# Window attention on one core: key differences with features on partitions, and value products summed by TensorE's turns

## The reference

```python
xw  = x.reshape(B, hg, ws, wg, ws, C).transpose(0, 1, 3, 2, 4, 5)     # windows of 2 x 2 positions
qkv = (xw @ Wqkv + bqkv).reshape(B, hg * wg, ws * ws, 3, nh, hd)      # 8 heads of 16 features
attn = softmax(einsum('bgnqd,bgnkd->bgnqk', q, k) * scale, axis=-1)   # 4 queries x 4 keys per window and head
o    = einsum('bgnqk,bgnkd->bgnqd', attn, v)
g = window_attn(xr) @ Wproj + bproj                                   # the full branch
l = resize(blur(window_attn(mean of 2x2 pixels)))                     # the pooled branch, bilinear, back to 32 x 32
out = x + (g + l).transpose(0, 3, 1, 2)
```

## Time and profile before

| | us |
|---|---|
| median of 3 runs | 103.97 |
| span of the profiled execution, first to last instruction | 101.1 |
| TensorE (PE) busy | 87.2 |
| VectorE (DVE) busy | 82.4 |
| GpSimd (POOL) busy | 51.4 |
| ScalarE (ACT) busy | 45.6 |

### The profile page before, as it was taken

How to read it: one execution, slowest core, us unless ns; L and a number is a source line. 1 busy time by engine, 2 the same in 40 slices (tenths; PEclk the granted TensorE clock), 3 DMA queues, 4 the chain that set the end, 5 groups by cost and what they waited for, 6 DMA issues and landing times.

```text
span 101.1 us, 1874 instructions
## 1 busy us (share of the span) xinstructions
PE 87.2 (86%) x647; PEld 79.8 (79%) x647; DVE 82.4 (81%) x137; ACT 45.6 (45%) x99; POOL 51.4 (51%) x43
## 2 busy tenths in 40 slices
PE   4949899989947998799999998589999994999960
PEld 1927589979947996799999996479999983999920
DVE  0062906999989999997979999999999999989770
ACT  3160247935862744864578505851613451222110
POOL 6201004499696930099999369729189549000000
PEclk9999999999998599999999999999999999999998
DMA  1699500000000000000000000005000004000072
GB/s 54 181 406 394 209 0 0 0 6 0 0 0 3 0 3 0 6 0 0 0 0 6 0 0 0 0 0 207 6 0 0 0 0 172 36 6 3 0 306 109
DMA packets 2313, 5.35 MB, mean 53 GB/s; under 512 B 513, under 2 KB 897, under 8 KB 2305
## 3 DMA queue, kind: packets, MB, share of 16 engines
q1 hardware_dynamic: 2016, 4.92, 12.7%
q10 hardware_dynamic: 288, 0.33, 1.1%
HBM read 3.15 MB, written 2.10 MB: 52 GB/s over the span
## 4 chain that ended last, share of the span: by engine, by line
PE 45%; DVE 21%; issue 13%; POOL 9%; DMA 5%; ACT 3%; SPq 0%; DVEq 0%; ACTq 0%; POOLq 0%
PE sm_ps L858 7%; PE ot_ps L882 6%; DVE sm_ps L674 6%; PE k_ps L823 6%; DMA x_sb<-in_x 5%; DVE qk L640 5%; POOL pv L387 5%; PE v_ps L847 5%; PE q_ps L823 3%; PE job_ps L802 2%; POOL qk L387 2%; PE ot_ps L776 2%; DVE out_sb L705 2%; PE v_ps L788 2%; PE ot_ps L788 2%
## 5 line engine op out<-in xcount | busy, mean ns | idle before, releaser
L387 POOL TENSOR_TENSOR pv<-pv 128x1024 f32<-128x1024 f32 (+1 forms) x11 | 21.6, 1964 | 8.3 <-DVE pv L691 7.9
L691 DVE TENSOR_TENSOR pv<-sm_ps,v_sb 128x2048 f32<-128x2048 f32 x9 | 20.6, 2290 | 0.3
L640 DVE TENSOR_TENSOR qk<-q_ps,k_sb 128x512 f32<-128x512 f32 x32 | 20.8, 679 | 0.0
L462 POOL TENSOR_TENSOR qk<-q_sb,k_sb 128x512 f32<-128x512 f32 x8 | 10.3, 1289 | 11.3 <-ACT q_sb L551 8.0
L387 POOL TENSOR_TENSOR qk<-qk 128x1024 f32<-128x1024 f32 (+1 forms) x7 | 15.5, 2217 | 0.2
L858 PE MATMUL sm_ps<-ident,qk 128*128 128x128 f32 x108 | 13.6, 274 | 1.3 <-POOL qk L387 1.2
L858 PEld LDWEIGHTS sm_ps<-ident,qk 128*128 128x128 f32 x108 | 11.9, 141 | 1.8 <-issue 1.7
L882 PE MATMUL ot_ps<-ident,pv 128*128 128x128 f32 x80 | 10.5, 274 | 2.5 <-POOL pv L387 1.9
L882 PEld LDWEIGHTS ot_ps<-ident,pv 128*128 128x128 f32 x80 | 9.0, 141 | 3.7 <-issue 3.3
L674 DVE TENSOR_TENSOR sm_ps<-expd,inv 128x128 f32<-128x128 f32 x10 | 10.1, 1011 | 0.3
L580 ACT ACTIVATE ot<-ot_ps,bias_v 128x512 f32<-128x512 f32 x10 | 6.9, 687 | 7.6 <-PE ot_ps L882 7.6
(11 more groups left out here) (88 smaller groups left out, 146.5 us busy)
## 6 DMA issues: line engine op xcount, KB each, us to landing
x_sb<-in_x SPq DMA_DIRECT2D x3, 512.0 KB, 7.1
out<-out_sb SPq DMA_DIRECT2D x3, 512.0 KB, 2.6
resize_sb<-in_resize SPq DMA_DIRECT2D x1, 640.0 KB, 7.3
x_sb<-in_x SPq DMA_DIRECT2D x2, 256.0 KB, 4.9
out<-out_sb SPq DMA_DIRECT2D x2, 256.0 KB, 2.0
w_sb<-in_L_conv_Wqkv ACTq DMA_DIRECT2D x1, 192.0 KB, 5.6
bias_rows<-in_L_conv_bqkv ACTq DMA_DIRECT2D x1, 128.0 KB, 4.6
wp_sb<-in_L_conv_Wproj SPq DMA_DIRECT2D x1, 64.0 KB, 6.6
```

What stands on the lines that cost most here:

```text
L387: return engine.tensor_tensor(low, low, high, ALU.add)
L462: nc.gpsimd.tensor_tensor(*query_key_operands(n, i, q_sb[:, n % 2, :], i - WIN + POOL_QUERIES), ALU.mult).then_inc(qk_pool, 1)
L640: ins = nc.vector.tensor_tensor(*query_key_operands(n, i, q_ps[n % 2][:, :], i), ALU.mult)
L691: nc.vector.tensor_tensor(to, a, b, ALU.mult).then_inc(pv_dve, 1)
```

## The change

The whole kernel is laid out anew. Images are taken in pairs, and a pair's four token positions (`j`) of a window are made separately. The normalised tokens of positions 1 to 3 have a reference token subtracted: keys and values are then computed as differences to those of position 0 (a softmax doesn't change when one key's score is taken from all, and the probabilities add up to 1, so the value of key 0 is added once). Three keys instead of four are multiplied, and no bias is needed for keys.

`K` and `Q` now have the weights as the stationary operand and give **features on the partitions**, with one product each of 384 and 512 columns. `M` is one VectorE instruction per tile, 12x128 = 1536 elements, reading the keys in PSUM. `S` handles two tiles: a product with 32 stationary columns sums features into heads; there are 4 queries x 4 groups of 32 windows, each of 192 columns, and each group writes its own 32 partitions. Row 0 of the scores (key 0) is zero, written once (`zero`). Softmax `X`, `D` handles two tiles at a time, 256 columns; probabilities get windows on the partitions by two VectorE transposes of 32x32 blocks. `P` is 1536 elements, reading the values in PSUM. `O` sums over keys by 4 turns per query, 16 per tile, in all ten tiles; GpSimd halves nothing. GpSimd pools the images for the pooled branch and does three normalisations; `lt` becomes 6 products per pair with mixing matrices. The input is loaded in pair layout, and once more (`xc`) for the residual. All `out` jobs have one bank, and there are four stores of a whole image.

```diff
-TILES = [(0, 0), (0, 1), (None, 0), (1, 0), (1, 1), (2, 0), (None, 1), (2, 1), (3, 0), (3, 1)]
+TILES = [(0, 0), (0, 1), (1, 0), (1, 1), (None, 0), (None, 1), (2, 0), (2, 1), (3, 0), (3, 1)]
...
     "DVE": [
...
+        ("M", 8), ("M", 9), ("out", 0, 0), ("P", 6), ("X", 4), ("out", 0, 1), ("P", 7), ("D", 4), ("out", 1, 0),
+        ("P", 8), ("out", 1, 1), ("out", 2, 0), ("P", 9), ("out", 2, 1), ("out", 3, 0), ("out", 3, 1),
...
     "POOL": [
...
+        ("std", 0), ("std", 1), ("pool", 0), ("pool", 1), ("pool", 2), ("pool", 3), ("lowmix",), ("std", 2),
+        ("norm", 1, 1), ("norm", 1, 2), ("norm", 1, 3),
...
+            def query_key(n):
...
+                shape = [P, WIN, KEYS, NW]
+                q = q_sb[:, n % QBUF, :].rearrange("f (q w) -> f q w", q=WIN).unsqueeze(2).broadcast_to(shape)
+                k = k_ps[n % 2][:, 0:KEYS * NW].rearrange("f (k w) -> f k w", k=KEYS).unsqueeze(1).broadcast_to(shape)
+                nc.vector.tensor_tensor(qk[:, m % 2, :, :, n % 2, :], q, k, ALU.mult).then_inc(qk_done, 1)
...
+            def keys(n):
...
+                nc.tensor.matmul(to, w_sb[:, C:2 * C], all_tokens(n, 1), start=True, stop=True).then_inc(k_made, 1)
...
             def sum_scores(n):
-                products_done(pe, n)
-                terms = HD >> sums_halved(pe, ("HS", "HS2"), n)
...
-                for d in range(terms):
-                    ins = nc.tensor.matmul(sm_ps[n % 2][:, ST], qk[:, n % 2, d * NS:(d + 1) * NS], ident[:, :],
-                                           is_transpose=True, start=(d == 0), stop=(d == terms - 1))
+                pe.wait_ge(qk_done, 2 * m + 2)
...
+                for q in range(WIN):
+                    for g in range(4):
+                        rows = slice(32 * g, 32 * (g + 1))
+                        ins = nc.tensor.matmul(s_ps[rows, 64:256], head_sum[:, q, :], qk[:, m % 2, q, :, :, rows],
+                                               start=(q == 0), stop=(q == WIN - 1), skip_group_check=True)
...
             def sum_values(n):
...
-                terms = WIN >> sums_halved(pe, ("HV", "HV2"), n)
+                terms = [0, 1, 2]
...
+                for q in range(WIN):
+                    to = view[:, q // 2, q % 2]
+                    nc.tensor.matmul(to, v0_sb[:, n % V0BUF, :], eye, is_transpose=True, start=True, stop=False,
+                                     skip_group_check=True)
+                    for k in terms:
+                        ins = nc.tensor.matmul(to, pv[:, n % 2, q, k, :], eye, is_transpose=True, start=False,
+                                               stop=(k == terms[-1]), skip_group_check=True)
```

More of the change, by code:

```diff
@@ L43 @@
 F32 = mybir.dt.float32
-BF16 = mybir.dt.bfloat16
 B, C, H, W = 4, 128, 32, 32
@@ L244, in conv_attention_kernel @@
         job_ps = psum("job_ps")
-        ST, SC, PR = slice(0, TILE_W), slice(TILE_W, TILE_W + NS), slice(2 * NS, 3 * NS)
         x0_rest = sem("x0_rest")
[L249 to L252, removed]
+        x_loaded = [sem(f"x_loaded{t}") for t in range(4)]
@@ L278, in among @@
             return [j for j in order if j[0] in kinds]
[L280 to L285 removed]
+        JOBS = among(ORDER["PE"], ("mean", "var", "xt", "lt", "out"))
         ACT_JOBS = among(ORDER["ACT"], ("xt", "lt"))
[L287 to L325 removed]
+        DVE_JOBS = among(ORDER["DVE"], ("mean", "var", "out"))
+        def bank(job):
+            if job[0] in ("mean", "var"):
+                return v_ps[1]
+            if job in (("xt", 0, 0), ("xt", 0, 2)):
+                return ot_ps
             return job_ps
@@ new lines, in jobs_read, with key_sums @@
+        def jobs_read(eng, item, its_bank):
+            jobs = [j for j in among(ORDER["PE"][:ORDER["PE"].index(item)], ("mean", "var", "xt", "lt", "out"))
+                    if bank(j) is its_bank]
+            if jobs:
+                job_read(eng, jobs[-1])
+        def key_sums(eng, kinds, n):
+            times = 0
+            for kind in kinds:
+                for e in ("POOL", "DVE"):
+                    if (kind, n) in ORDER[e]:
+                        eng.wait_ge(summed[e, kind], sum(j[0] == kind and j[1] <= n for j in ORDER[e]))
+                        times += 1
+            return times
@@ L688, in prob_value @@
-                to, a, b = (pv[:, n % 2, :].rearrange("w (q kh d) -> w q kh d", q=WIN, d=HD),
-                            p.unsqueeze(3).broadcast_to(shape), v.unsqueeze(1).broadcast_to(shape))
-                if n < N - 1:
-                    nc.vector.tensor_tensor(to, a, b, ALU.mult).then_inc(pv_dve, 1)
-                else:
-                    for q in range(WIN):
-                        nc.vector.tensor_tensor(to[:, q], a[:, q], b[:, q], ALU.mult).then_inc(pv_last, 1)
-            def result(job):
-                kind, b, half = job
-                cs = {"out": slice(0, C), "begin": slice(0, CH), "end": slice(CH, C)}[kind]
+                shape = [P, WIN, KEYS * HEADS, HD]
@@ L722, in _ @@
             PE = ORDER["PE"]
-            OUT_FIRST = among(PE, ("out", "low"))[0]
-            def jobs_read(item, its_bank):
-                jobs = [j for j in among(PE[:PE.index(item)], ("xt", "lt")) if bank(j) is its_bank]
-                if jobs:
-                    job_read(pe, jobs[-1])
-            def job_begins(job):
-                earlier = [j for j in JOBS[:JOBS.index(job)] if bank(j) is bank(job) and j[0] != "low"]
-                if earlier:
-                    job_read(pe, earlier[-1])
+            OUT_FIRST = among(PE, ("out",))[0]
@@ L737, in do_job @@
+            K_FIRST = among(PE, ("K",))[0]
+            def job_begins(job):
+                its_bank = bank(job)
+                jobs_read(pe, job, its_bank)
+                at = PE.index(job)
+                if its_bank is ot_ps:
+                    done = len(among(PE[:at], ("O",)))
+                    if done:
+                        pe.wait_ge(ot_out, done)
             def do_job(job):
                 job_begins(job)
-                values_before, values_summed = before(PE, job, ("V",)), before(PE, job, ("O",))
@@ L772, in do_job @@
[L772 to L789 removed]
+                    _, p, j = job
@@ L790, in do_job @@
                 else:
                     _, b, half = job
-                    low = POOLED[b // 2]
-                    tiles = [TILES.index((b, t)) for t in range(HALVES)]
-                    if kind in ("out", "low"):
-                        blocks = [i for i, (k, _) in enumerate(BLOCKS) if k // (K // 2) == half]
-                        pe.wait_ge(ot_out, low + 1)
-                        for i in blocks:
-                            k, l = BLOCKS[i]
-                            at = (k - half * K // 2) * C
-                            low_ot = ot[:, low, :].rearrange("f (b l c) -> f b l c", b=2, l=KL)[:, b % 2, l]
-                            ins = nc.tensor.matmul(bank(job)[:, at:at + C], resize_sb[:, i, :], low_ot,
-                                                   start=(i == blocks[0]), stop=True, skip_group_check=True)
@@ L804, in do_job @@
-                    for t in {"low": (), "out": (0, 1), "begin": (0,), "end": (1,)}[kind]:
-                        pe.wait_ge(ot_out, tiles[t] + 1)
-                        ins = nc.tensor.matmul(
-                            bank(job)[:, :].rearrange("f (k t c) -> f t k c", t=HALVES, c=CH)[:, t], wp_sb[:, :],
-                            ot[:, tiles[t], :].rearrange("f (h k c) -> f h k c", h=2, c=CH)[:, half],
-                            start=False, stop=True, skip_group_check=True)
+                    low, tile = TILES.index((None, b // 2)), TILES.index((b, half))
@@ new lines, in do_job @@
+                    if job == OUT_FIRST:
+                        pe.wait_ge(wp_loaded, 16)
+                        pe.wait_ge(resize_loaded, 16)
+                    used = [i for i, (k, _) in enumerate(BLOCKS) if k // (K // 2) == half]
+                    pe.wait_ge(ot_out, low + 1)
+                    for i in used:
+                        k, l = BLOCKS[i]
+                        at = (k - half * K // 2) * C
+                        low_ot = ot[:, low, :].rearrange("f (b l c) -> f b l c", b=2, l=KL)[:, b % 2, l]
+                        nc.tensor.matmul(to[:, at:at + C], resize_sb[:, i, :], low_ot, start=(i == used[0]), stop=True,
+                                         skip_group_check=True)
@@ L827, in keys, with all_tokens @@
-            def keys(n):
-                pe.wait_ge(k_seeded, n + 1)
-                product(n, 1, k_ps).then_inc(k_made, 1)
+                for j in range(WIN):
+                    job_read(pe, ("lt", half) if b is None else ("xt", b // 2, j))
+            def all_tokens(n, first):
+                b, half = TILES[n]
+                if b is None:
+                    return xl[:, half, first * NW:]
+                return xt_view[:, b // 2, first:, b % 2, half]
+            def keys(n):
+                if ("K", n) == K_FIRST:
+                    pe.wait_ge(w_loaded, 16)
```

(5 more changed lines are left out.)

773 lines of the change are left out of this document (361 added, 412 removed), and 48 rows, old and new, of the table ORDER.

## The result

The changed kernel takes 114.7 us, median of 4 runs (113.23 to 115.31), and the kernel before on the same chip 104.06 (103.12 to 104.32): 1.1012 times as long, 95% interval 1.0912 to 1.1111. Some executions of a kernel are over 1.5% longer than its fastest; ratios and intervals are of the others, medians and ranges of all. The forecast was 116 and slower, so it held.

A forecast was written before the change was run, and what follows sets the result against it. TensorE and VectorE were both taken as full in the body, with TensorE deciding after the second sum. The fifth sum at 78.2, tail, residual, store and 1.0 for the clock gave span 113.4, plus 2.87: 116 us, range 107 to 130.

The forecast's parts named there:

- the sum of scores: TensorE's 32 instructions per group of two tiles: half overlap between column slices, 2.7 us per group.
- 17 steps: Sum of scores: a product's second instruction runs beside the next product's first, so 17 x 0.161 = 2.7 us.
- rival (c): Sum of scores: all four slices overlap fully, 1.29 us per sum, 109 us in all, still slower; chance 17%.
- (b): Sum of scores: no overlap, 5.15 us per sum, five sums at 2.45 more, 128 us in all; chance 31%.
- the 0.6 for GpSimd's pooling: Start: wait added to three normalising instructions because they run beside GpSimd's pooling; 0.6 us, bounds 0 to 1.3.
- charged for the clock: Start: allowance for first products and first sum running at the low clock; 1.0 us, bounds 0 and 4.2.
- the forecast's own terms from 14.6 to the last copy: Start: normalising 0.54, 0.75, 0.75, plus 0.6, last `xt` 0.44, copy 0.59; said to end at 19.2.
- First to second sum: Body, from one sum's start to the next: VectorE's order decides, 10.4 us.
- The tail's waits: TensorE after the fifth sum: 7.0 us, with 1.9 for the bank and 2.0 for the exponential behind `V` 8.
- the four that were put near 1.0: Tail: four waits near 1.0 us each, for the single banks of `out` and `O`.
- VectorE's wait ahead of each `X`: Sign that would show the forecast: VectorE idle 3 us or more ahead of each softmax step `X`.
- Rival (d): Body: VectorE decides, loses 15 us and GpSimd's lock, so time falls to 95 us; chance 8%.

The follow-up runs named there:

- experiment 1: Changed kernel with the column slice as outer loop of the sum of scores, so neighbouring products share a slice: 122.94 us, ratio 1.1836 to the kernel before.
- experiment 4: Changed kernel with GpSimd's pooling waiting for VectorE's last normalising instruction of the first pair: 112.31 us, ratio 1.0837 to the kernel before.
- after: The changed kernel with the whole new layout, against the kernel before: 114.7 us, 1.1012 times as long.
- experiment 5: Changed kernel with the first residual job of images 1, 2 and 3 in the queries' idle bank: 108.69 us, ratio 1.0474 to the kernel before.
- experiment 6: Changed kernel with ScalarE's last exponential ahead of the copy of tile 8's values: 111.1 us, ratio 1.0703 to the kernel before.
- experiment 10: Changed kernel with late pooling, two banks for out jobs, last exponential first, late bias loads and filler products together: 105.69 us.
- experiment 12: Changed kernel with late pooling, second out bank, earlier exponential, late bias loads, filler products, GpSimd additions replacing turns, tile 8's turns in a keys bank: 100.45 us.

## Why the prediction was right, and where it was not

**Outcome and place.** The forecast said that VectorE's gain of 15 us would not count, because TensorE decides after the second sum and start and tail grow. So it went: VectorE fell from 82.4 to 65.9 (67 predicted), TensorE was busy for 36.3 of 38 us from the second sum to the fifth, and the span grew.

**The step that failed: the sum of scores**, forecast at 2.7 us and measured at 1.44. Its mechanism, overlap in part, held; both factors in it were mis-sized. The price of one instruction was taken from 256 dense columns scaled to 192, 0.161; experiment 1 measured 0.108, and 17 steps of that are 1.84. This is the larger miss, 0.9 us per sum. The overlap was put at two instructions, 32 in the time of 17; it is 2.4-fold with four slices in turn, which takes another 0.4. The number of rival (c), 1.29, lies nearest, but by luck: full overlap at the measured price would be 0.87. Against the rule of the Trainium skill, TensorEngine Tiling, Tiling Modes, which was weighed there, the trace agrees in direction, at 2.4 times and not four. No overlap (b) would with the measured price have been 3.46 per sum and not 5.15: about 125, and 122.94 as the median of experiment 1, not 128.

**The start was undercounted.** From `mv` to the first sum 19.4 was forecast (7.41 to 26.8) and 23.27 came. The normalisation took 3.83 (17.69 to 21.52) where 2.64 were summed: the 0.6 for GpSimd's pooling should have been the 1.8 of experiment 4, above even its upper bound of 1.3, because L504 was thought free of it. The products of the start ran slowly: the first eight turns took 1.96 where 16 in 1.75 make 0.88, and the last transposes, `K` and `Q` cost 0.66, 0.97 and 0.86 over their dense prices, 3.6 together, where 1.0 was charged for the clock. Against that the forecast's own terms from 14.6 to the last copy add up to 18.3 and not to the 19.2 that stands there, so 0.9 was charged without a term. And the second piece of the image landed 1.84 us later in this execution than in before's, which no edit explains.

**First to second sum.** The forecast let VectorE's order decide there. In the chain of after TensorE does, with `K`, `Q`, `V` and the products of `lt`; with the measured sum the forecast would be 9.1, and 10.04 came.

**The ledger of the span**, from 113.4 forecast: five sums at 1.26 less, -6.3; start +3.9, less the 1.0 already charged; landing +1.8; the stretches between the sums, apart from the sums, +1.6 (48.0 from first to fifth sum against 51.4 forecast, and 5.0 of that is the sums); the tail apart from its sum -0.7. That makes 112.7, the measured span. So a right total rests on -6.3 and +5.6 that cancel, which is luck. With the sums right and the rest as forecast the number would have been about 110, too low by more than the runs scatter.

**What held.** `O` 16 turns in 1.75, `K` 0.65, `Q` 0.86, `V` 0.89, `M` and `P`, `D` with 2.17 for 1.95; the stretches from second to fifth sum within 0.4 us each once the sum's price is put right (12.27, 11.60 and 14.09 against 12.14, 11.24 and 13.84). The tail's waits were forecast at 7.0 and are 6.7 in the chain, and the two main ones were named: the bank behind the residual (experiment 5) and the exponential behind `V` 8 (experiment 6). The second is 3.4 and not 2.0, and of the four that were put near 1.0 there are two, 0.86 and 0.82. The two causes overlap, since 4.9 was won by the first alone. VectorE's wait ahead of each `X` was 6.6 for five, where 3 or more *each* was said to show the forecast; the sum that it waits for was 1.3 us shorter. Rival (d), VectorE decides, did not happen: from after to experiment 10 VectorE's work falls by 1.9 us (to 64.0) and the time by 9.

**What stays open.** Why four slices give 2.4 and not 4; why one instruction of 32 columns costs 0.108 and not 0.161; why TensorE runs at half rate behind the first sum in seven of the thirteen profiled executions of the new layout, whether the first `K` was slow or not; what moves the landing of the second piece, apart from the bias loads.

## What to carry to other kernels

Before you price a small product by a large one, look whether it uses the whole array: products in different column slices, issued in turn, run beside each other, and the order of two loops is worth 8 us by the medians here and 10 by the stretches. When two engines' work falls and the time rises, measure start, body and tail apart. From after to experiment 12 the span falls by 15.0: 8.2 in the tail (the bank, the exponential, turns given back to GpSimd), 4.1 in the start (pooling behind the normalisation, filler products), 1.8 in the body and 2.6 in the landing, less 1.6 lost behind the first sum. In the body TensorE is first, but the others are close behind: of 5.2 us of turns taken off it, 1.8 were won. Check a forecast that came out right by its terms; this one had errors of about 6 us of both signs.

## What the runs showed of the hardware

- Products of 32 weight columns and 192 moving columns advance the chain by 0.108 us each when all use one slice, 0.066 with two slices in turn and 0.045 with four; at 96 columns and one slice 0.058.
- The granted clock in a profile can miss a stretch at half rate. After's first `K` and `Q` took 1.62 and 1.72 us, about twice the 0.84 and 0.86 of the next ones, in a stretch whose clock column says 1.00; in experiment 5 the same products took 1.62 and 1.72, and the column there says 0.50:

```profile
22.00:24.00 2.00, 2.00 (x4) 1.01 (x3) 0.00 (x0) 0.00 (x0) 1.92 (x5) 0.50 0.00 0
```

- A VectorE instruction with one large input from SBUF, L504, took 1.25 us beside GpSimd's pooling (after) and 0.55 without it (experiment 4).
- The landing of the same image load varies: the statistics (`mv`) began between 6.90 and 9.25 us in nine kernels, and between 6.33 and 6.68 in the four whose bias loads are issued after the image has landed.
